# Attention and routed experts on one core: the batch loop written out, and the normalising activations spread over a slot

## The reference

```python
h = layernorm(x)
q, k, v = split(h @ W_attn)               # 16 heads of 8 channels
q, k = rope(q), rope(k)
att = softmax(causal(q @ k.T / sqrt(8)))
x = x + (att @ v) @ W_proj
h = layernorm(x)
gates = sinkhorn(h @ gate_w, 8 rounds)    # 8 experts
for each expert: top 64 tokens by gate    # the last writer of a token wins
    y[token] = (h[token] @ experts[e]) * (gate > 0.5)
out = x + y
```

## Time and profile before

| what | value |
|---|---|
| time of the kernel | 546.09 us, median of 3 runs (544.55 to 549.57) |
| the profiled execution | 553.09 us |
| its span, first to last instruction | 551.4 us |
| mean granted clock of TensorE | 0.912 |
| PE / DVE / ACT / POOL busy | 428.1 / 417.9 / 332.6 / 230.2 us |

### The profile page before, as it was taken

The page is one execution under the profiler, slowest core; times in us unless marked ns, Lnnn a source line. Parts: engine busy times, 40 slices in busy tenths (PEclk is TensorE's granted clock), DMA queues, the critical chain, the costliest instruction groups (busy, mean ns, idle before and its releaser), DMA issues.

```text
span 551.4 us, 11207 instructions
## 1 busy us (share of the span) xinstructions
PE 428.1 (78%) x2857; PEld 214.1 (39%) x2857; DVE 417.9 (76%) x1693; ACT 332.6 (60%) x660; POOL 230.2 (42%) x399
## 2 busy tenths in 40 slices
PE   0508989988989898998989899899987778898200
PEld 0202444454444445445444554445543433333100
DVE  7768759787778768877777887778951599989980
ACT  0103668678777658877775887778793334328613
POOL 5031544363364236346424634643342000009997
PEclk9955879999998999999899999989999799899855
DMA  8570161035026004402600530360010100101111
GB/s 253 153 171 0 51 158 24 1 127 124 2 96 136 23 0 150 97 1 103 130 18 19 145 84 0 115 133 2 2 58 0 39 19 21 38 0 39 44 44 47
DMA packets 28172, 36.72 MB, mean 67 GB/s; under 512 B 2080, under 2 KB 24160, under 8 KB 26464
## 3 DMA queue, kind: packets, MB, share of 16 engines
q1 hardware_dynamic: 27184, 34.68, 23.0%
q10 hardware_dynamic: 944, 1.57, 1.1%
HBM read 19.41 MB, written 16.78 MB: 66 GB/s over the span
## 4 chain that ended last, share of the span: by engine, by line
PE 48%; DVE 15%; ACT 10%; issue 10%; POOL 10%; DMA 4%; DVEq 1%; POOLq 1%; ACTq 1%; SPq 0%
PE ROWB L446 11%; PE CHB L459 10%; PE PVB L471 9%; PE MB L503 5%; PE MB L479 5%; ACT YS L700 4%; POOL SUM L846 4%; POOL SUM L844 3%; PE MB L513 3%; DMA YS<-parts_scratch 3%; DVE JUNK L893 2%; PE ROWB L641 2%; DMA parts_scratch<-PARTS 2%; ACT XN L679 1%; PE MB L492 1%
## 5 line engine op out<-in xcount | busy, mean ns | idle before, releaser
L893 DVE CUSTOM_DVE_ANT_0 JUNK<-ROWB,TRI 128x384 bf16<-128x384 f32 (+3 forms) x512 | 221.5, 487 | 37.9 <-PE ROWB L446 36.1
L700 ACT ACTIVATE YS<-CHB 128x512 f32<-128x512 f32 x320 | 172.7, 607 | 59.4 <-PE CHB L459 58.6
L810 POOL TENSOR_SCALAR_AFFINE_SELECT YS<-YS 128x256 f32<-128x256 f32 x256 | 104.4, 412 | 179.4 <-ACT YS L700 171.1
L446 PE MATMUL ROWB<-YS 96*128 96x384 bf16 (+3 forms) x512 | 124.6, 317 | 25.3 <-DMA YS<-parts_scratch 18.5
L459 PE MATMUL CHB<-YS 104*128 104x384 bf16 (+3 forms) x512 | 119.4, 310 | 13.7 <-ACT YS L700 10.9
L471 PE MATMUL PVB<-YS,VP 128*32 128x512 f32 (+3 forms) x1024 | 97.4, 454 | 0.2 <-POOL YS L810 0.2
L446 PEld LDWEIGHTS ROWB<-YS 96*128 96x128 bf16 x512 | 43.7, 101 | 104.4 <-DVE MX L893 49.5
L459 PEld LDWEIGHTS CHB<-YS 104*128 104x128 bf16 x512 | 46.5, 100 | 48.9 <-ACT YS L700 19.6
L769 ACT ACTIVATE YS<-YS,W 128x128 f32<-128x128 f32 x104 | 31.5, 389 | 34.5 <-POOL SUM L844 18.9
L654 ACT ACTIVATE YS<-MB 8x1024 bf16<-8x1024 bf16 x32 | 32.5, 1016 | 32.7 <-PE MB L492 32.5
L471 PEld LDWEIGHTS PVB<-YS,VP 128*32 128x32 f32 x1024 | 35.5, 111 | 27.7 <-POOL YS L810 13.3
(11 more groups left out here) (124 smaller groups left out, 557.1 us busy)
## 6 DMA issues: line engine op xcount, KB each, us to landing
YS<-parts_scratch SPq DMA_DIRECT2D x30, 384.0 KB, 6.4
parts_scratch<-PARTS SPq DMA_DIRECT2D x15, 384.0 KB, 2.5
parts_scratch<-PARTS SPq DMA_DIRECT2D x15, 256.0 KB, 2.2
X<-in_x SPq DMA_DIRECT2D x8, 256.0 KB, 5.4
xn_scratch<-XN2S SPq DMA_DIRECT2D x8, 256.0 KB, 2.0
XS<-xn_scratch SPq DMA_DIRECT2D x8, 256.0 KB, 2.7
out<-X SPq DMA_DIRECT2D x8, 256.0 KB, 2.3
parts_scratch<-PARTS SPq DMA_DIRECT2D x15, 128.0 KB, 1.8
```

What stands on the lines that cost most here:

```text
L446: last = pe.matmul(ROWP[BANK[u]][:, col:col + keys], QP[par][0:ROWS_K, pair, P * qb:keys], KZ[par][i % 2][0:ROWS_K, pair, 0:keys], start=T ...
L700: act.activation(PT[s % 2][:, c, :], CH[BANK[c]], ACT.Exp).then_inc(exp_done, 1)
L810: pool.affine_select(out=v, in_=v, pattern=[[0, 2], [1, P]], compare_op=ALU.is_ge, fill=0.0, base=0, channel_multiplier=-1).then_inc(causa ...
L893: last = dve.tensor_tensor_reduce(out=JUNK[BANK[u]][:, col:col + n], in0=ROWP[BANK[u]][:, col:col + n], in1=TRI[:, T - n:T], scale=1.0, sc ...
```

## The change

The loop is replaced by eight batches written out, on every engine, with constants in place of registers. `normalize_x` and `normalize_x2` now write one tile per call. The tiles of XN follow the exponentials of c4, c5, c6 and c7 in slot 3, for batch b + 2 (that of batch 1 is written ahead of batch 0). The tiles of XN2 follow the exponentials of c4, c5, c6 and c7 in slot 2, still for batch b - 1.

```diff
-NORMALIZE = (0, "w", 9)
+NORMALIZE = {(3, "c", 4 + t): t for t in range(TB)}
...
-NORMALIZE2 = (2, "u", 6)
+NORMALIZE2 = {(2, "c", 4 + t): t for t in range(TB)}
...
-            one(Batch(0, 0, prev=False))
-            with eng.Fori(1, B - 2, 2) as i:
-                one(Batch(i, 1))
-                one(Batch(i + 1, 0))
-            one(Batch(B - 1, 1, nxt=False))
+            for b in range(B):
+                one(Batch(b, b % 2, prev=b > 0, nxt=b < B - 1))
...
-            def normalize_x(b):
-
-                for t in range(TB):
-                    tile = bass.ds(TB * b + t, 1)
-                    last = act.activation(XN[:, t, :], X[:, tile, :].rearrange("p a c -> p (a c)"), ACT.Identity,
-                                          scale=RSTD[:, tile], bias=SHIFT[:, tile])
-                last.then_inc(xn_ready, 1)
-
-            def normalize_x2(b):
-
-                act.wait_ge(ln2_rstd, b + 1)
-                for t in range(TB):
-                    last = act.activation(XN2[:, t, :], X[:, bass.ds(TB * b + t, 1), :].rearrange("p a c -> p (a c)"),
-                                          ACT.Identity, scale=RSTD2[:, t:t + 1], bias=SHIFT2[:, t:t + 1])
-                last.then_inc(xn2_ready, 1)
+            def normalize_x(b, t):
+
+                tile = slice(TB * b + t, TB * b + t + 1)
+                last = act.activation(XN[:, t, :], X[:, TB * b + t, :], ACT.Identity, scale=RSTD[:, tile],
+                                      bias=SHIFT[:, tile])
+                if t == TB - 1:
+                    last.then_inc(xn_ready, 1)
+
+            def normalize_x2(b, t):
+
+                if t == 0:
+                    act.wait_ge(ln2_rstd, b + 1)
+                last = act.activation(XN2[:, t, :], X[:, TB * b + t, :], ACT.Identity, scale=RSTD2[:, t:t + 1],
+                                      bias=SHIFT2[:, t:t + 1])
+                if t == TB - 1:
+                    last.then_inc(xn2_ready, 1)
...
             def one(bt):
+                b = bt.b
                 for s in range(4):
...
-                        if bt.nxt and (s, kind, i) == NORMALIZE:
-                            normalize_x(bt.b + 1)
-                        if bt.prev and (s, kind, i) == NORMALIZE2:
-                            normalize_x2(bt.b - 1)
+                        if b + 2 < B and (s, kind, i) in NORMALIZE:
+                            normalize_x(b + 2, NORMALIZE[s, kind, i])
+                        if bt.prev and (s, kind, i) in NORMALIZE2:
+                            normalize_x2(b - 1, NORMALIZE2[s, kind, i])
 
             act.wait_ge(ln_rstd, 2)
+            for t in range(TB):
+                normalize_x(1, t)
             batches(act, one)
...
-            normalize_x2(B - 1)
+            for t in range(TB):
+                normalize_x2(B - 1, t)
```

## The result

The changed kernel takes 559.89 us, median of 4 executions (558.35 to 560.69); the kernel before took 547.83 beside it. The ratio is 1.021, with a 95% interval of 1.013 to 1.029. Measured once more, 6 executions against 11: 560.98 against 546.80 us, ratio 1.026 (1.0225 to 1.030). It is slower by 12 to 14 us, where I forecast 5.8, at 551.9, and a range up to 559.

The account below looks back on a forecast made before the run. PE's order of work was taken to set the pace. Terms -5.97 - 0.84 + 7.55 + 3.8 gave +4.5 us, 550.6 on the median of 546.09; with 1.3 added, 551.9 us, range 542 to 559.

Parts of the forecast that it names:

- On the median it gives 550.6: Whole kernel: +4.5 us applied to the median of the runs before, 546.09, instead of the profiled execution, 553.1.
- third of the 4.6: Slot 2: near 1.3 us added because a run before may lack the three falls of the clock, worth 4.6.
- slots 3 (jumps gone, XN moved): Slot 3 and loop end: two jumps back removed, -5.97 us, and XN moved from slot 0, -0.84.
- slots 2, the delay: Slot 2: PE's transposes wait 1.18 us longer for XN2's fourth tile, seven batches, +8.26; less batch 1's DMA wait, +7.55.
- slots 2, falls of the clock: Slot 2: pauses of 2.4 us bring six falls in seven batches at 1.4 each, +8.4, less three present: +3.8 us.
- the loop written out: Loop end: both jumps back go, 3.04 and 2.93 us, -5.97; registers turned into constants and longer code 0.
- XN moved: Slots 0 and 3: -0.70 us without the block, +0.56 in slot 3, net -0.14 at six boundaries, -0.84.
- XN2 late: Slot 2: XN2's fourth tile ready at 227.4, transposes start 1.18 us later in seven batches; with batch 1's wait, +7.55.
- The price of a fall: Slot 2: each fall of the clock costs 1.4 us, bounded by seven at 1.53.
- Rival B: Slot 2: the clock stays up despite the longer pauses, -3.9 us, giving 542.2; chance 0.17.
- D: Batches 3 to 6: fetching the longer program stops 2.39 us in each, +9.6, at most 561.5; chance 0.07.
- E: Loop end: the 3 us are not in the jump and recur in straight code, +6.0, giving 557.9; chance 0.05.

Follow-up runs that it names:

- unroll_only: Changed kernel with both normalisations, XN and XN2, put back at their old places as blocks, batches still written out: 544.36 us, ratio to before 0.995.
- unroll_xn: Changed kernel with XN2 put back as a block in slot 2, XN still spread over slot 3: 542.23 us, ratio to before 0.992.
- warm_wait: Changed kernel with ten products nobody reads ahead of PE's wait for XN2's fourth tile in slot 2: 550.20 us, ratio to before 1.005.
- late_xn2t: Changed kernel with PE's transposes of XN2 moved from x4 of slot 2 to x1 of slot 3, logits to x3: 545.90 us, ratio 0.998.
- unroll_xn2: Changed kernel with XN put back as a block in slot 0, XN2 still spread over slot 2: 561.17 us, ratio to before 1.029.
- loop_xn2: Kernel before, loop kept, with only XN2 spread over c4 to c7 of slot 2: 563.44 us against 548.26, ratio 1.032.
- warm_before: Kernel before with four products nobody reads ahead of PE's wait at c5 of slot 2: 546.28 us against 548.37, ratio 0.997.
- early_tiles: Changed kernel with XN2's tiles behind the exponentials of c1, c2, c4 and c5 of slot 2: 541.91 us, ratio 0.989.

## Why the prediction was wrong

The step that failed is the one from the profiled execution to the median: "On the median it gives 550.6", with 1.3 us added. For the profiled execution I forecast 557.6 us, and it took 559.36, 1.8 more. From there I went down 5.7 us (7.0 less 1.3), because the profiled execution of the kernel before lay 7.0 us above its median. The changed kernel has no such distance: its two profiled executions, 559.36 and 560.57, lie 0.5 and 0.4 us below its medians, 559.89 and 560.98. That is 6.2 of the 8.0 us between 551.9 and 559.89.

The distance belonged to the kernel before, as the second trace of it shows: all three falls in slot 2 were a draw, and so was one of those at the jumps, where 12.30 - 9.47 and 10.84 - 9.47 are 4.2 us together, not 5.97. I had written that falls come and go, but carried this to both kernels, as if the falls that I forecast for the changed one would stay away as often. They don't: its mean granted clock was 0.898 to 0.908 in the six executions of its larger sample, that of the kernel before 0.912 to 0.927 in the eleven beside them. (Two slips of the prediction change little: the "third of the 4.6" is 1.5 and not 1.3, and the second of the two pauses at the jumps is 1.79 and not 2.00.)

The other 1.8 us are what two larger errors leave of each other. The two traces, slot by slot, as the sum for the profiled execution had it:

| term | forecast | measured |
|---|---|---|
| slots 3 (jumps gone, XN moved) | -6.8 | -6.9 |
| slots 2, the delay | +7.55 | +8.1 |
| slots 2, falls of the clock (four, 6.1 us, for three, 4.7) | +3.8 | +1.4 |
| slots 0 and 1 | 0 | +0.4 |
| ahead of c0 of batch 0, and from c0 of (7, 3) to the end | 0 | +3.0 |
| sum | +4.5 | +6.0 |

That +4.5 came near +6.0 is luck: too many falls (six for four) stand against the parts outside the stage, for which I had no term. In medians the terms are these:

| term | forecast | measured | from |
|---|---|---|---|
| the loop written out | -5.97 | -3.1 | unroll_only - before |
| XN moved | -0.84 | -2.1 | unroll_xn - unroll_only |
| XN2 late | +7.55 | +8.0 | warm_wait - unroll_xn |
| falls of the clock | +3.8 and +1.3 | +10.8 | changed kernel (560.98) - warm_wait |
| sum | +5.8 | +13.6 | |

The kernels were measured on different chips, where the kernel before had medians from 546.8 to 548.4, so each row is good to 1 or 2 us only. The forecast for the falls counts against those that the kernel before has, the 10.8 against a kernel with none in slot 2; the falls that the kernel before has in its median stand mostly in the first row.

*Right: the mechanism and the schedule.* Slot 3 was forecast at 9.3 and takes 9.34; slot 2 at 11.5 and takes 11.59; the transposes were to start 1.18 us later and start 1.28 later (6.11 - 4.83); the wait was to be 2.3 to 2.5 us, seven times, and is 2.4. The DMA wait of batch 1 vanished behind the delay. From c0 of batch 3 to c0 of batch 4 I forecast about 48 us, and it takes 48.1. That registers and straight code cost nothing in the stage held.

*The price of a fall* was right for the usual one, 1.4 us against 1.4 to 1.6 in seven of the eight in the two traces of the changed kernel, but not as a bound. I had built it on the one length that the trace before showed, and the fall of 16.02 us shows that one can last through most of a slot, for 4.43. With 1.50, 1.38 and 1.44 for the other three, the second trace of the changed kernel has 8.8 us of falls in slot 2 alone.

*A term left out: the stretch from c0's exponential in slot 3 of batch 7 to the end.* In the trace of the changed kernel it takes 557.4 - 413.7 = 143.7 us, against 551.4 - 410.3 = 141.1 before, with the code untouched but for one call. Two windows of it at 1.2 GHz, of the changed kernel:

```profile
431.40:441.60 10.20, 7.37 (x21) 4.80 (x21) 4.59 (x15) 2.14 (x3) 0.00 (x0) 0.50 0.07 26
482.60:489.40 6.80, 5.63 (x14) 2.37 (x15) 5.21 (x17) 0.00 (x0) 0.00 (x0) 0.50 0.00 2
```

In the trace before, the first ended after 6.83 us; in the second trace of the kernel before this is the only one of its kind, and the stretch takes 140.0 us:

```profile
422.57:429.40 6.83, 4.74 (x15) 3.56 (x16) 3.79 (x13) 0.72 (x1) 0.00 (x0) 0.50 0.11 40
```

Over all twelve traces the length goes with the time at 1.2 GHz in this stretch (the last 32 to 36 us left out, where the clock is low in every trace): 140.0 and 140.1 us with 6.8 us of it, 141.1 with 10.2, 142.1 to 142.9 with 13.7, 143.7 to 143.8 with 17.1; only late_xn2t, 144.3 with 13.7, stands apart. In the seven written-out kernels with PE's transposes in their place it takes 142.5 to 143.8 us, in the four looped ones 140.0 to 142.1. Why the clock is low for longer in the former, and whether that is chance, stays open.

Rival B (the clock stays up) is refuted for a wait of 2.39 us on ACT, which brings falls in most batches; with the same wait filled with products that nobody reads there are none. The Trainium skill ("TensorE: Matmul & The Clock Gate", HAM oscillation) describes such falls for waits on transfers. D and E did not occur: the gaps of "issue" are absent, and slot 3 takes 9.34 us in straight code. The chance of 0.50 on slower was on the right side. The upper end of 559 was too low because it was rival E's 557.9 with a little on top: like the forecast, it contained the 5.7 us taken off on the way to the median.

## What to carry to other kernels

Spreading an engine's work thinly is free only if the last piece still comes before its reader needs it: look for the reader's place in its own engine's order, not at the busy share of the writer. Where the trace shows TensorE's clock falling, price a new pause above its length, and bound it by more than the usual fall. Take several profiles of the kernel before, since one profiled execution may have all of the falls or none, and do not carry the distance between its profiled execution and its median over to the changed kernel. In the kernel with the long pauses, filling them with products that nobody reads won 10.8 us; in the kernel before, with pauses of 1.18 us, no gain was clear of noise.

## What was not expected of the hardware

How often PE's granted clock fell to 1.2 GHz in the slot of a pause, counted in the traces (batches 1 to 7 for slot 2):

| PE's pause | falls | traces |
|---|---|---|
| 2.4 us, slot 2 | 18 of 28 | changed kernel (two), unroll_xn2, loop_xn2 |
| 1.8 to 2.0 us, at a jump back | 3 of 8 | kernel before (two), loop_xn2, warm_before |
| 1.18 us, slot 2 | 6 of 28 | kernel before (two), unroll_only, unroll_xn |
| 0.72 us, slot 2 | 0 of 7 | early_tiles |
| filled with products | 0 of 14 | warm_wait, warm_before |

So a fall came more often with a longer pause, and never in every case; and one trace with none shows little: the kernel before had 3 of 7 in one trace and 0 of 7 in the other. In the two traces of the changed kernel a fall cost 1.4 to 1.6 us in seven cases and 4.43 in one. A loop's jump back, with DVE idle for some 2.2 to 2.4 us over its own instructions, cost 1.34 to 1.45 us in the five cases where the clock stayed up, one of them in warm_before:

```profile
181.13:192.05 10.92, 9.04 (x83) 5.11 (x82) 7.86 (x38) 8.37 (x18) 3.25 (x8) 1.00 0.01 3
```
